# Second layer's tables loaded in the gate's block, and the first four token tiles of the shared expert split there

## What is computed

```python
x = x + ssm0(ctx, layernorm(x))        # in_proj, conv of 4, x_proj, scan over 16 states, D, silu gate
x = x + moe(layernorm(x))              # router softmax, top 4 of 16, shared expert * sigmoid
x = x + ssm1(ctx, layernorm(x))
x = x + ternary_ffn(layernorm(x))
# moe:
shared = (silu_and_mul(x @ shared_gate_up_w.T) @ shared_down_w.T) * sigmoid(x @ sgate_w.T)
coef_e = sum(where(topk_ids == e, topk_w, 0)); out = shared + sum_e coef_e * expert_e(x)
```

## Time and profile before

| | |
|---|---|
| median of three runs | 2118.13 us |
| the profiled execution, its own time | 2118.25 us |
| its span (first to last instruction) | 2116.4 us |
| PE / DVE / ACT / POOL busy | 76% / 81% / 55% / 63% |
| mean granted TensorE clock | 0.90 |
| first block, second, third (by the timeline) | 0 to 635, 635 to 759, from 759 us |

### The profile page before, as it was taken

One profiled execution on the slowest core, in us unless ns is written; L12 is line 12 of the kernel. 1 busy time (PEld: TensorE's weight loads), 2 busy tenths in 40 slices (PEclk: granted clock), 3 DMA queues, 4 the chain that ended last, 5 costly groups with the idle time before them and its releaser, 6 DMA issues. The chain is left out here.

```text
span 2116.4 us, 26823 instructions
## 1 busy us (share of the span) xinstructions
PE 1618.6 (76%) x8338; PEld 916.9 (43%) x8338; DVE 1715.7 (81%) x2270; ACT 1169.4 (55%) x1798; POOL 1330.6 (63%) x645
## 2 busy tenths in 40 slices
PE   4675765766664558888888898999999999067788
PEld 1222222322224435666566555666655665023344
DVE  3999999999967656998599947888658887678876
ACT  5676776676643116655666535455354444146576
POOL 2689878788973002998099915888418887654221
PEclk7788988889986569999999999999999999579999
DMA  6646546446547122432333243545445642642200
GB/s 212 231 160 229 203 144 217 161 149 197 179 139 267 63 76 89 142 120 78 120 115 105 89 173 132 186 155 199 152 156 180 230 142 77 197 121 61 74 16 31
DMA packets 130517, 305.19 MB, mean 144 GB/s; under 512 B 23856, under 2 KB 33328, under 8 KB 126288
## 3 DMA queue, kind: packets, MB, share of 16 engines
q1 hardware_dynamic: 86800, 206.33, 28.8%
q10 hardware_dynamic: 32144, 59.65, 8.0%
q0 software_dynamic: 11440, 37.50, 6.0%
HBM read 215.09 MB, written 88.34 MB: 143 GB/s over the span
## 5 line engine op out<-in xcount | busy, mean ns | idle before, releaser
L494 POOL TENSOR_TENSOR ssm_hs<-ssm_hs,ssm_Cs 128x1024 f32<-128x1024 f32 x128 | 313.9, 2464 | 90.6 <-DVE ssm_hs L461 90.6
L494 POOL TENSOR_TENSOR moe_hs<-moe_hs,moe_Cs 128x1024 f32<-128x1024 f32 x128 | 301.6, 2356 | 48.9 <-DVE moe_hs L461 48.0
L461 DVE TENSOR_TENSOR_SCAN moe_hs<-moe_dA,moe_bu 128x1024 f32<-128x1024 f32 x128 | 292.5, 2285 | 21.1 <-ACT moe_dA L375 13.0
L484 POOL TENSOR_TENSOR moe_U<-moe_U,moe_hs 128x1024 f32<-128x1024 f32 x128 | 301.9, 2359 | 6.4
L1446 PE MATMUL moe_pgu<-all_Wreg,moe_xt 128*128 x1896 | 301.0, 312 | 0.0
L461 DVE TENSOR_TENSOR_SCAN ssm_hs<-ssm_dA,ssm_bu 128x1024 f32<-128x1024 f32 x128 | 291.5, 2278 | 0.1
L294 PE MATMUL ssm_pY<-ssm_hs,ssm_ident 128*128 128x512 f32 x512 | 278.4, 671 | 8.1 <-POOL ssm_hs L494 7.9
L1396 PE MATMUL moe_pgu<-all_Wreg 128*128 128x256 f16 x2112 | 250.9, 276 | 13.9 <-DVE moe_hsl L1647 13.9
L1396 PEld LDWEIGHTS moe_pgu<-all_Wreg 128*128 128x128 f16 x2112 | 208.9, 99 | 62.1 <-issue 13.7
L1446 PEld LDWEIGHTS moe_pgu<-all_Wreg,moe_xt 128*128 128x128 f16 x1896 | 185.4, 98 | 94.7 <-issue 2.3
L747 POOL TENSOR_TENSOR ssm_wlo<-ssm_wst,ssm_whi 128x1360 f16<-128x1360 f32 (+2 forms) x63 | 188.5, 2991 | 34.1 <-ACT ssm_wst L682 34.1
(11 more groups left out here) (272 smaller groups left out, 3212.1 us busy)
## 6 DMA issues: line engine op xcount, KB each, us to landing
ssm_wst<-in_w_all SPq DMA_DIRECT2D x51, 680.0 KB, 5.2
y_d<-moe_yo ACTq DMA_DIRECT2D x79, 256.0 KB
all_Wreg<-w_hi SPq DMA_DIRECT2D x16, 1088.0 KB
all_Wreg<-w_lo SPq DMA_DIRECT2D x16, 1088.0 KB
w_hi<-ssm_whi SPq DMA_DIRECT2D x51, 340.0 KB, 2.3
w_lo<-ssm_wlo SPq DMA_DIRECT2D x51, 340.0 KB, 3.1
ssm_Cs<-c_d SPq DMA_DIRECT2D x64, 256.0 KB, 5.5
moe_Cs<-c_d ACTq DMA_DIRECT2D x64, 256.0 KB, 3.9
```

What stands on the lines that cost most here:

```text
L461: self.nc.vector.tensor_tensor_scan(self.hs[:, j, :, :].rearrange("p k t -> p (k t)"), self.dA[:, q, :, :].rearrange("p k t -> p (k t)"), ...
L484: self.nc.gpsimd.tensor_tensor(Y, Y, self.hs[:, j, :, :], ALU.add).then_inc(self.acc_done, 1)
L494: self.nc.gpsimd.tensor_tensor(self.hs[:, j, :, :], self.hs[:, j, :, :], self.Cs[:, i:i + 1, :].to_broadcast([P, HC, L]), ALU.mult)\
```

## The change

The ten tables and `cx` of the second layer become objects of the whole program (`Weights`), and the second block's SyncE queue loads the ten ahead of `wr` and `cx` behind the first four `w_sh` pieces; TensorE waits there for the ten tables before its first transpose. The gate uses the same `ident`. When the router is done, ScalarE writes the high parts of the four tiles that lie in `xT` (12 to 15) and scales `xT` in place, and GpSimd subtracts to get the low parts. The third block's units take the tiles in the order 12 to 15, 0 to 11: the first four need no load, transpose or split, the two preliminary ones and those of slots 4 and 7 fall away, and `sh_up(0)` goes ahead of `pe_in(0, 0)`. The four semaphores of the split are set by hand at the start.

```diff
+class Weights:                       # the ten tables, cx, and their two semaphores
+    def load(self, sp): ...          # the ten DMAs, as before
+    def load_ctx(self, sp, b): ...
 # gate_and_routing, SyncE
-                sp.dma_start(ident[:], d["ident"]).then_inc(loaded, 16)
+                w1.load(sp)
                 sp.dma_start(wr[:], d["w_router"].rearrange("(k p) n -> p k n", p=P)).then_inc(loaded, 16)
...
                 for c in range(4):
                     shared(c)
+                w1.load_ctx(sp, 0)
 # gate_and_routing, ScalarE, behind the sigmoid
+                for i in range(FIRST):
+                    t, q = divmod(i, 2)
+                    nc.scalar.activation(xsh[:, t, :, q * P:(q + 1) * P], xT[:, i, :, :], ACT.Copy, scale=XS).then_inc(hi_rdy, 1)
+                for i in range(FIRST):
+                    act.wait_ge(hi_rdy, i + 1)
+                    nc.scalar.activation(xT[:, i, :, :], xT[:, i, :, :], ACT.Copy, scale=XS).then_inc(xs_rdy, 1)
 # gate_and_routing, GpSimd, behind the products
+                for i in range(FIRST):
+                    t, q = divmod(i, 2)
+                    pool.wait_ge(xs_rdy, i + 1)
+                    nc.gpsimd.tensor_tensor(xsl[:, t, :, q * P:(q + 1) * P], xT[:, i, :, :], xsh[:, t, :, q * P:(q + 1) * P],
+                                            ALU.subtract).then_inc(xl_rdy, 1)
 # gate_and_routing, TensorE
-                pe.wait_ge(loaded, 32)
+                pe.wait_ge(w1.loaded, 160)
+                pe.wait_ge(loaded, 16)
 # experts_and_ssm
+        def tile(i):
+            return (i + TT - FIRST) % TT
 # SyncE
-                load_shared(0)
-                load_shared(1)
-                S.load_ctx(sp, 0)
-                S.load(sp)
-                load_shared(2)
-                load_shared(3)
+                load_shared(FIRST)
+                load_shared(FIRST + 1)
                 Q.sp_load(sp, 0)
                 Q.sp_load(sp, 1)
 # TensorE
                 S.pe_start(pe)
-                sx_transpose(0)
-                sx_transpose(1)
+                pe.sem_inc(sx_tr, FIRST)
+                sh_up(0)
                 S.pe_in(pe, 0, 0)
...
-                        sh_up(slot)
+                        if slot:
+                            sh_up(slot)
 # ScalarE, VectorE: sx_high(0), (1) and sx_low(0), (1) removed, sem_inc by FIRST in their place
 # in the slots, for TensorE, ScalarE and VectorE alike
-                        if c in XT and t + 1 < NTS:
+                        if c in XT and FIRST <= 2 * (t + 1) + XT.index(c) < TT:
 # VectorE, where a pair's result is added to X
-                        i = 2 * t + q
+                        i = tile(2 * t + q)
```

More of the change, by code:

```diff
@@ L78, in last_row, with split_tokens @@
     return r["Wreg"][:, o:o + IF].bitcast(BF16)
+def split_tokens(r):
+    return [r["Wreg"][:, XSH + z * 2 * HK * TS:XSH + (z + 1) * 2 * HK * TS].rearrange("p (t k n) -> p t k n", t=2, k=HK)
+            for z in range(2)]
 class Mem:
@@ L103, in _, with __init__, load, load_ctx @@
                     sp.sem_clear(s)
+class Weights:
+    def __init__(self, m, l, d):
+        self.l, self.d = l, d
+        self.sel = m.sb(f"sel{l}", [96, NS, P], BF16)
+        self.cx = m.sb(f"cx{l}", [P, 2, L])
+        self.w_in = m.sb(f"w_in{l}", [P, 2, DI])
+        self.w_x = m.sb(f"w_x{l}", [P, KC, 96 + DR])
+        self.w_up = m.sb(f"w_up{l}", [P, DI])
+        self.cw = m.sb(f"cw{l}", [P, KC, DC])
+        self.cb = m.sb(f"cb{l}", [P, KC])
+        self.db = m.sb(f"db{l}", [P, KC])
+        self.alog = m.sb(f"alog{l}", [P, KC, NS])
+        self.Dv = m.sb(f"Dv{l}", [P, KC])
+        self.ident = m.sb(f"ident{l}", [P, P])
+        self.loaded = m.sem(f"loaded{l}")
+        self.cx_in = m.sem(f"cx_in{l}")
+    def load(self, sp):
+        d, l = self.d, self.l
+        for dst, src in [(self.ident[:], d["ident"]), (self.sel[:], d["sel"][:, 0:NS, :]),
+                         (self.w_in[:], d[f"w_in{l}"].rearrange("(k p) n -> p k n", p=P)),
+                         (self.w_x[:], d[f"w_x{l}"].rearrange("(k p) n -> p k n", p=P)),
+                         (self.w_up[96:96 + DR, :], d[f"w_up{l}"]),
+                         (self.cw[:], d[f"cw{l}"].rearrange("(k p) n -> p k n", p=P)),
+                         (self.cb[:], d[f"cb{l}"]), (self.db[:], d[f"db{l}"]), (self.Dv[:], d[f"D{l}"]),
+                         (self.alog[:], d[f"alog{l}"].rearrange("(k p) n -> p k n", p=P))]:
+            sp.dma_start(dst, src).then_inc(self.loaded, 16)
+    def load_ctx(self, sp, b):
+        sp.dma_start(self.cx[:], self.d["ctxT"].rearrange("(k p) n -> p k n", p=P)[:, :, b * L:(b + 1) * L])\
+          .then_inc(self.cx_in, 16)
@@ L106, with __init__ @@
 class Ssm:
-    def __init__(self, nc, m, l, d, dbl, ring, alone):
+    def __init__(self, nc, m, w, d, dbl, ring, alone):
         self.alone = alone
[L119 to L128, removed]
+        self.nc, self.w, self.d, self.dbl, self.ring = nc, w, d, dbl, ring
+        self.sel, self.cx, self.w_in, self.w_x, self.w_up = w.sel, w.cx, w.w_in, w.w_x, w.w_up
+        self.cw, self.cb, self.db, self.alog, self.Dv, self.ident = w.cw, w.cb, w.db, w.alog, w.Dv, w.ident
+        self.loaded, self.cx_in = w.loaded, w.cx_in
@@ L204, in bank_dt @@
         return self.bank(b, c + 1 if self.alone else c)
[L206 to L216, removed]
     def load_ctx(self, sp, b):
[L219 to L222, removed]
+        sp.wait_ge(self.in_rdy, KC * b)
+        self.w.load_ctx(sp, b)
     def store_y(self, sp, y_ssm, b):
@@ L505, in ssm_first @@
         m = Mem(nc, ctx, "ssm0")
-        S = Ssm(nc, m, 0, d, dbl=2, ring=R, alone=True)
+        w0 = Weights(m, 0, d)
+        S = Ssm(nc, m, w0, d, dbl=2, ring=R, alone=True)
         NST = B * STEPS
@@ L573, in _ @@
             def _(sp):
-                S.load(sp)
-                S.load_ctx(sp, 0)
+                w0.load(sp)
+                w0.load_ctx(sp, 0)
                 for j in range(2):
@@ L1229, in experts_and_ssm @@
         sigs = m.sb("sigs", [P, TT])
-        xsh, xsl = [Wreg[:, XSH + z * 2 * HK * TS:XSH + (z + 1) * 2 * HK * TS].rearrange("p (t k n) -> p t k n", t=2, k=HK)
-                    for z in range(2)]
+        xsh, xsl = split_tokens(r)
         sgs = m.sb("sgs", [P, 2, IE])
```

37 lines of the change are left out of this document (18 added, 19 removed).

## The result

The changed kernel takes 2108.53 us in the median of 7 runs (2104.65 to 2114.68), beside 2120.63 us (2117.39 to 2125.71, 7 runs) for the kernel before on the same chip: ratio 0.9951, interval 0.9939 to 0.9963: faster, by half a percent (the ratio on record is worked out from all the runs; the quotient of the two medians alone is 0.9943). One further run of the changed kernel, in e8, took 5290 us, two and a half times all others, and is left out wherever e8 is used. The profiled execution took 2108.07 us with a span of 2106.0 us, 10.4 us less than the 2116.4 of before.

A forecast was written before the change was run, and what follows sets the result against it. The prediction took TensorE's 15.3 us wait for the last of ten tables at the third block's start as the bound. Terms -13.4 + 3.8 - 1.2 + 0.1 = -10.7 against 2118.25 gave 2107.5 us, range 2103 to 2112.

The forecast's parts named there:

- The start: Third block's start up to `pe_in(0, 2)`: tables' wait and two transposes go, a gain of 13.4 us.
- best case: Third block, TensorE's start to `pe_in(0, 2)`: 9.6 us if the clock comes up after 3.6 us of work.
- The split beside the routing: Gate's routing: GpSimd's four subtractions hold VectorE's masks and sums with two SBUF inputs, costing 3.8 us.
- VectorE getting nothing in between two GpSimd operations: Routing: reading of the L909 row, where 0.16 us became 2.50; reason for taking +3.8, near the upper end 4.9.
- Slots 4 and 7: Third block's slots 4 and 7: transposes and low parts fall away, 0.6 us each, -1.2 in all.
- The gate's front: Gate's start: nine more tables ahead of `wr`, `cx` behind four `w_sh` pieces, costed at 0.
- covered by 3 to 6 us: Gate's front: `wr` lands at 649 to 652, TensorE needs it at 655.06.
- if the cover is gone, each us late is a us at 655: Gate's front: without cover, every us of lateness is lost at TensorE's first transposes.
- What comes behind: Slots after the start: chained to one another, so the start's gain should reach the program's end; no term.
- VectorE gets the port first: Rival in the routing, chance 0.10: GpSimd pays instead, +1 in place of +3.8, giving 2104.7 us.
- Part of the gain is taken back: Rival, chance 0.10: gate opens late or third block starts slowly, 2 to 5 us, giving 2109.5 to 2112.5.

The follow-up runs named there:

- e8: The changed kernel run once more, unaltered, to see what varies between executions: 2107.47 us in the median of three runs, ratio 0.9937.
- e2: The changed kernel with ScalarE's split tile by tile, two tiles ahead of the logits' copy and two behind the sigmoid: 2105.89 us, ratio 0.9925.
- e3: The changed kernel with GpSimd's four subtractions held back until VectorE reaches its 64 one-hot pairs: 2109.03 us, ratio 0.9943.
- e6: The changed kernel with cx (512 KB) at the very front of the gate's SyncE queue, so wr comes later: 2103.16 us in one run.
- e9: The changed kernel with GpSimd's four subtractions replaced by memsets of the low parts to zero: 2106.74 us in one run.
- e7: The changed kernel with the tiles' half alone: ten tables and cx loaded at the third block's start, as before the change: 2117.18 us, ratio 0.9996.

## Why the forecast was right, step by step

Forecast 2107.5 in a range of 2103 to 2112, measured 2108.53.

- **The start**: -13.4 forecast, -14.0 measured. Both waits and both transposes went as worked out. The gap behind the gate was 3.14 us (762.26 - 759.12) where I had 2.85, and from TensorE's first matmul to the mark it took 9.44 us, as in the best case (9.6), not the 10.3 that I took: the clock came up within the unit, which took 4.24 us. That was the shortest of six executions with this start (this one, e2, e3, e6, e8, e9): the unit took 4.24 to 5.28 us, and the mark lay between 12.58 and 13.72, a gain of 12.9 to 14.0, in the mean 13.5. That the token tiles' own DMA was a second wait behind the tables I did not see; it costs the sum nothing, because the change takes both away, but it is 2.4 of the 3.7 us by which the tiles are worth more here than in e7.
- **The split beside the routing**: +3.8 forecast, +3.0 measured, with place and mechanism right (e2 takes it away by time, e9 by taking away GpSimd's reads). Mis-sized was the step "VectorE getting nothing in between two GpSimd operations": at L981 they took turns, one wait of about 0.9 us for each of three masks. At L909 itself the forecast's reading holds in every execution, so one row of one operation did not carry over to another place. ScalarE's operations took 0.54, not 0.6, so GpSimd began at 714.4 instead of 715.2, and the first subtraction met the search for indices and a cast, not a mask.
- **Slots 4 and 7**: -1.2 forecast, -0.95 measured.
- **The gate's front**: 0 forecast, 0 measured, but for another reason than mine; "covered by 3 to 6 us" was wrong. The step that failed is the issue time: 6.4 us for ten tables came from a stretch with a DMA share of 0.62, and at a share of 1.01 SyncE needed 10.0 us for them. `wr` itself then took 9.7 us to land, at the 7 to 10 that I had assumed. "if the cover is gone, each us late is a us at 655" was wrong too, and this saved the term: VectorE waits at L935 for GpSimd's last product in any case. In e6 2.3 us of lateness were gone at 35.1 us after the gate's start, before the router's first matmul.
- **What comes behind**: 0 forecast, +2.1 in the profiled execution, 1.7 of it TensorE's clock in the second prologue, which e8 doesn't have but five of the other changed versions do. The prediction put this at nothing; whether it belongs to the change stays open. The gate itself up to the logits gave 0.4, its start 0.1: -14.0 + 3.0 - 0.95 - 0.4 - 0.1 + 2.1 = -10.4.

So the forecast's -10.7 meets -10.4 partly by offsets: by the first scan the kernel stood at -12.5, 1.8 better than worked out, and most of that went again in the second prologue, for a reason that isn't settled. That the two nearly cancel is luck. With the mean start the landmarks give -13.5 + 3.0 - 0.95 = -11.4, with the second prologue's loss -9.7; the interval of the ratio is 7.8 to 12.9 us of gain and doesn't tell them apart. Of the rivals, "VectorE gets the port first" did not occur at its price (+1): there were turns, but they cost 3.0. "Part of the gain is taken back" named 2 to 5 us from the gate's opening or the third block's start; the gate's opening lost nothing and the start met the forecast. What was lost lay elsewhere.

## What to carry to other kernels

When a wait is removed, look up when each other input of the same instructions was issued, for the next wait may lie hidden right behind it; two parts of a change that stand behind one wait are worth nothing or much, depending on which goes first. Give an idle GpSimd its work where VectorE does not run, or runs operations that a trace shows unharmed; small steps alone are no shelter. The same four subtractions cost 0 us ahead of the masks (two beside nothing, two beside index searches), 3.0 beside the masks and 3.7 beside f16 one-input operations. A cover that is computed from issue times of a quieter stretch does not hold where the DMA engines are full. Before counting each us of a late start as a us lost, look for the next wait that doesn't depend on it: here it took up 2.3 us.

## What the runs showed of the hardware

- GpSimd and VectorE can alternate, operation by operation: three masks of four waited about 0.9 us each, and two subtractions of four took 1.33 us in place of 1.15. At L909, L935 in the changed kernel, one VectorE operation on 4 columns always ended with GpSimd's last product and stood 2.1 to 2.5 us, longer than one product of 1.23 (0.37 in e6, where it began late). What decides between the two was not tried.
- Small f16 operations with one tensor input (TENSOR_SCALAR) are held by GpSimd's subtractions as well: 0.24 and 0.29 us became 1.2. FIND_INDEX8, 0.17 us, kept its time beside them.
- SyncE's issue of a small table took 0.43 to 1.39 us at a DMA share of 0.62, up to 2.94 at 1.01, and in e6 up to 4.75 at 0.89.
- One program differs between executions where TensorE's granted clock does. The first unit of the third block took 4.24 us at a granted clock of 0.62 and 5.28 at 0.50 (e3) with the same start; the last 32 router matmuls took 3.94 us in the one execution of the changed kernel (0.69 from 700 to 709 us) and 6.85 in the other (0.50 from 700 to 714). The last stage took 298.0 to 302.9 us over all the kernels here, though none of them changes it; why was not looked into. A difference of a few us between two single profiles means nothing unless its rows show the step that made it.
